# A four-layer graph network on one core: two banks for the gathered rows, signals counted by quads, and sum and one-hots of a quad in one step

## The chip, the cores and the metric

The kernel runs on one core of one Trainium2 chip. The number that counts is the device time of a whole execution in microseconds; lower is better. Engines are named as in the profile: PE is TensorE (PEld its weight loads), DVE is VectorE, ACT is ScalarE, POOL is GpSimd, SP is SyncE.

## What is computed

12,500 nodes with 128 features each, 212,500 edges sorted by destination, and four graph layers one after the other, each of the form x = x + layer(relu(layernorm(x))). Every layer is a product of the nodes with small weights and one or two sums over the edges. Cut to what matters:

```python
# layer 0, twice (10 relations): mean over the edges of each (destination, relation)
sums = segment_sum(x[src], dst * NUM_REL + edge_type, N * NUM_REL)
cnt  = segment_sum(ones, dst * NUM_REL + edge_type, N * NUM_REL)
out  = einsum('nrd,rdo->no', (sums / max(cnt, 1)).reshape(N, NUM_REL, -1), w_rel) + x @ root + bias
# layer 1 (3 relations): one sum of table rows, weighted by the edge
hr = einsum('ni,rio->rno', feature, weight)
h  = segment_sum(hr[rel_type, src] * norm[:, None], dst, N)
# layer 2, twice: mean over the in-edges
agg = segment_sum(h[src], dst, N) / max(deg, 1)[:, None]
h   = agg @ Wl.T + bl + h @ Wr.T
# layer 3: rows times a filter made from 20 edge features, summed by the other end of the edge
Wij = (ssp(f_ij @ W_filt1 + b_filt1) @ W_filt2 + b_filt2) * rcut_ij[:, None]
agg = segment_sum(h[idx_j] * Wij, idx_i, N)
```

## The kernel before

**Stages.** Dense stages and passes over the edges take turns. A dense stage reads the sums of the pass before (kept transposed in the SBUF tile `acc`, 128 features by 12,800 nodes), updates x and writes a table of rows to DRAM (`table_dram`). The seven passes are, in order, COUNT (pass 0, counts per relation, no table), LOOKUP (pass 1), four PLAIN passes (2 to 5) and FILTER (pass 6). Passes 1 to 5 are the gather passes: for each edge they fetch its table row. Pass 5 also prepares, for pass 6, where each edge's sum will be stored (`finds_dest`). The loop over repeats (`reps`) runs once for these inputs.

**One gather pass.** The edges are cut into 1664 tiles of 128, four tiles to a quad, four quads to a group, 104 groups. A group goes like this:

- POOL copies eight row numbers (`row_st` from `row_i`, L583), waits for the copy (`row_staged`), and issues eight indirect DMAs (L588), each of which fetches 128 rows of 512 bytes into one tile of `rows`; then the same for the other eight tiles. `rows` holds one group. So before each half POOL waits until PE has used the same half of the group before: `mm_done`, which PE raises by one after each tile.
- DVE waits until PE has done the whole group before, copies the destinations and weights of the group (`rw_st`, L1015 and L1032), and builds sixteen 128x128 one-hot tiles `hot` (they live in the tile `tab_s`), L1038: column n of edge e is the edge's weight if e goes to node n of the quad's window, else zero. Each raises `hot_ready` by one.
- PE waits for a quad's rows (`row_in[q]`) and one-hots and sums `rows` times `hot` over four tiles in one PSUM bank (L734; an f32 product is issued as two matmuls).
- DVE adds each quad's PSUM bank to a window of `acc` (L997) and raises `add_done` by four.

In the PLAIN passes DVE's order within a group is all sixteen one-hots and then the four additions. The LOOKUP pass is longer: an edge's weight (one over the count of its destination and relation) is not known yet. PE transposes small relation one-hots (L791), ACT copies them (L682), PE looks up the counts with them (L801, L803), and DVE multiplies and reduces each tile twice, first for the degree and then for the relation (`weigh`, L1050, an operation and the read of its accumulator), the second in place over `hot`. In pass 5 DVE also compares every tile's sources with each other (`pairs`, L1069, and their reduction, L1080), on rows that SP loads from DRAM by quads (`src_row`, L456).

**FILTER.** Pass 6 has its own order; POOL scatters with adding (L570), 16 tiles a group, each with waits of its own.

**What sets the order.** Everything is written out by hand: every engine runs its own loops, and semaphores with running counts join them. `settle` is a semaphore increment by the engine's sequencer after a wait.

Of the kernel before, what the change touches and what calls it, by code (L numbers as in the profile page):

```python
# [28 lines left out]
P = 128  # L29
# [34 lines left out]
def build(nc, d, out, n_nodes, n_edges):  # L64
# [34 lines left out]

    with ExitStack() as ctx:  # L100
# [22 lines left out]
        scratch = sb("scratch", [P, max(nacc, 3 * GROUP * P + 8 * BANK + 2 * P, 2 * COPIES * SB)])  # L123
        src_i = sb("src_i", [P, ntiles], I32)
        row_i = sb("row_i", [P, ntiles], I32)
# [109 lines left out]
        row_in = [sem(f"row_in{q}") for q in range(4)]  # L235
# [81 lines left out]
        def tiles_before(reps, pn):  # L317

            return reps * (pn * ntiles)

        def windows(e, g):
# [3 lines left out]
                skip_runtime_bounds_check_because="a destination or the start of a window of nodes, from 0 to n_nodes")[1]  # L325

# [58 lines left out]
        def _(sp):  # L385
# [10 lines left out]
            sp.wait_ge(add_done, reps * ntiles + GROUP)  # L396
# [11 lines left out]
            for k, p in enumerate(DENSE):  # L408
# [40 lines left out]
                if k == 1:  # L449
                    sp.wait_ge(add_done, reps * (3 * ntiles) + GROUP)  # L450
# [8 lines left out]
                if k == 4:  # L459
                    sp.wait_ge(add_done, tiles_before(reps, 5) + GROUP)  # L460
# [5 lines left out]
                if k == 5:  # L466

                    sp.wait_ge(add_done, tiles_before(reps, 6) + GROUP)
# [36 lines left out]
        def _(pool):  # L505
# [28 lines left out]
            for k, p in enumerate(DENSE):  # L534
# [21 lines left out]
                if PASSES[k + 1] != FILTER:  # L556
                    pool.wait_ge(rows_ready, sum(q in (0, 2, 3) for q in range(k + 1)))
                else:

                    with pool.Fori(0, reps) as r:  # L560
                        with pool.Fori(0, ngroups) as g:
                            n0 = pool.snap((r * ngroups + g) * 4)
                            base = pool.snap(tiles_before(reps, 6) + n0 * QUAD)
                            for q in range(4):
                                pool.wait_ge(dest_ready, n0 + (q + 2))
                                pool.wait_ge(add_done, base + (GROUP + QUAD * (q + 1)))
# [144 lines left out]
        def _(pe):  # L711
# [25 lines left out]
            def gathered(base, q):  # L737

                pe.wait_ge(row_in[q], base + 64)
# [166 lines left out]
        def _(dve):  # L906
# [92 lines left out]
            def run_pass(pn):  # L999
# [7 lines left out]
                with dve.Fori(0, reps) as r:  # L1007
                    set_windows(pn, r)
                    with dve.Fori(0, ngroups) as g:
# [89 lines left out]
                        if kind == LOOKUP:  # L1099
                            for u in range(GROUP):  # L1100
                                one_hot(u)
# [236 lines left out]
```

## Time and profile before

| | us |
|---|---|
| median of three runs | 18440.12 |
| lowest and highest run | 18428.23, 18442.12 |
| span of the profiled execution | 18422.2 |
| PE, DVE, ACT, POOL busy in it | 8433.5, 7139.1, 2442.5, 11077.2 |

The span runs from the first to the last instruction of the profiled execution; the median lies 17.9 us above it. Busy time counts the instructions themselves, not semaphore waits or register work. In rows with square brackets these hold the idle time just before the instruction and what ended it; such rows begin with the start and the duration. Rows of groups give busy time, the mean in ns of one, the idle time just before them and what ended it. Rows of waits give the total, how often, and the longest. A releaser "remote" means that no instruction of this core was found that ended the wait at that time; "issue" means that the profile shows nothing that was waited for.

### The profile page before, as it was taken

What the parts mean: (1) busy time and instruction counts of PE and PEld (TensorE: products, weight loads), DVE (VectorE), ACT (ScalarE), POOL (GpSimd) and SP (SyncE); (2) the same over time, 40 slices, a digit from 0 to 9 for tenths busy, and PEclk for the clock granted to TensorE, in tenths of its full rate; (3) what the DMA queues carried; (4) which work ended last, traced back from release to release, by engine and by line L of the source; (5) the groups of instructions that cost most, each with busy time, mean ns of one, the idle gap of its engine ahead of it and who ended that gap; (6) DMA issues with size and microseconds to landing.
All of it is one profiled execution on the core that took longest, in us unless ns stands there. A gap on an engine that the chain in (4) does not pass through costs nothing. (4 is left out here: it accounts for less than half of the span.)

```text
span 18422.2 us, 189911 instructions
## 1 busy us (share of the span) xinstructions
PE 8433.5 (46%) x37745; PEld 6706.7 (36%) x37746; DVE 7139.1 (39%) x33414; ACT 2442.5 (13%) x4374; POOL 11077.2 (60%) x11347
## 2 busy tenths in 40 slices
PE   2464444463333343333343333333333377777777
PEld 1233333333333333333332332322222355555555
DVE  7644444432222232222232222255555534444443
ACT  0120000020000020000020000000000044444443
POOL 0045555636666646666636666566666448888883
PEclk9975555585555565555565555555555567777775
DMA  2131111131111131111121111123333246666665
GB/s 85 64 123 40 40 39 39 40 146 55 45 45 45 45 100 45 45 45 45 45 66 45 45 45 45 49 80 84 83 84 84 73 95 118 118 117 118 117 117 122
DMA packets 981246, 1326.79 MB, mean 72 GB/s; under 512 B 201421, under 2 KB 635620, under 8 KB 981180
## 3 DMA queue, kind: packets, MB, share of 16 engines
q0 software_dynamic: 552016, 851.84, 21.1%
q1 hardware_dynamic: 429208, 474.72, 8.9%
q8 instruction: 6, 0.10, 0.0%
q14 instruction: 16, 0.13, 0.0%
HBM read 992.21 MB, written 333.54 MB: 72 GB/s over the span
## 5 line engine op out<-in xcount | busy, mean ns | idle before, releaser
L588 POOL DMA_INDIRECT rows<-table_dram,row_st x8320 | 8018.1, 964 | 3188.8 <-issue 2894.6
L734 PE MATMUL ps<-tab_s,rows 128*128 128x128 f32 x16640 | 4123.4, 427 | 6939.1 <-DMA rows<-table_dram,row_st 4302.8
L734 PEld LDWEIGHTS ps<-tab_s,rows 128*128 128x128 f32 x16640 | 3604.2, 320 | 7432.5 <-issue 7386.0
L570 POOL DMA_INDIRECT agg_dram<-acc,sum_row x1664 | 2646.9, 1591 | 529.0 <-issue 383.7
L997 DVE TENSOR_TENSOR acc<-ps,acc 128x128 f32 x2080 | 605.5, 291 | 5685.4 <-PE ps L734 4010.6
L1038 DVE TENSOR_SCALAR tab_s<-iota,rw_st 128x128 f32<-128x128 f32 x6656 | 1787.8, 361 | 11.5
L734 PE MATMUL ps<-scratch,tab_s 128*128 128x128 f32 x3328 | 669.0, 366 | 821.8 <-DVE scratch L1182 791.5
L583 POOL COPY row_st<-row_i 128x8 int32 x1040 | 210.5, 202 | 1262.7 <-PE ps L734 1072.4
L734 PEld LDWEIGHTS ps<-scratch,tab_s 128*128 128x128 f32 x3328 | 596.8, 269 | 871.7 <-issue 871.3
L548 POOL DMA_DIRECT2D table_dram<-tab_s x200 | 106.6, 533 | 1179.9 <-ACT tab_s L671 917.4
L635 ACT ACTIVATE yT<-acc 128x512 f32 x75 | 46.9, 626 | 4899.5 <-DVE acc L997 4893.7
L1176 DVE COPY sum_row<-etype 128x4 int32 x416 | 81.3, 195 | 1458.4 <-POOLq L569 1400.8
L1050 DVE CUSTOM_DVE_ANT_0 xs<-ps,tab_s 128x128 f32<-128x128 f32 x1664 | 385.1, 287 | 629.2 <-remote 446.2
L825 PE MATMUL ps<-scratch,acc 128*128 128x128 f32 x3328 | 593.3, 338 | 10.1 <-issue 5.9
L682 ACT ACTIVATE yT<-ps 128x512 bf16<-128x512 f32 x416 | 248.4, 597 | 2519.3 <-remote 1111.3
L1069 DVE TENSOR_SCALAR xn_h<-scratch,src_st 128x128 f32<-128x128 int32 x1664 | 377.5, 299 | 517.9 <-remote 392.0
L752 PE MATMUL ps<-scratch,wfilt 20*128 20x512 f32 x836 | 553.1, 745 | 35.0 <-DMA scratch<-in_feat 27.7
L825 PEld LDWEIGHTS ps<-scratch,acc 128*128 128x128 f32 x3328 | 559.2, 253 | 17.4 <-issue 17.4
L1050 DVE CUSTOM_DVE_ANT_0 tab_s<-ps,tab_s 128x128 f32<-128x128 f32 x1664 | 384.6, 287 | 457.5 <-remote 389.8
L551 POOL DMA_DIRECT2D table_dram<-tab_s x100 | 75.5, 755 | 795.6 <-ACT tab_s L671 609.7
L760 PEld LDWEIGHTS ps<-wfilt,scratch 128*128 128x128 f32 x3336 | 510.4, 219 | 15.8
L760 PE MATMUL ps<-wfilt,scratch 128*128 128x128 f32 x3336 | 507.3, 302 | 0.0
(182 smaller groups left out, 10596.4 us busy)
## 6 DMA issues: line engine op xcount, KB each, us to landing
scratch<-in_src_row SPq DMA_DIRECT2D x832, 256.0 KB
rows<-table_dram,row_st POOLq DMA_INDIRECT x8320
table_dram<-tab_s POOLq DMA_DIRECT2D x200, 640.0 KB, 3.2
scratch<-in_dst_row SPq DMA_DIRECT2D x416, 256.0 KB
scratch<-table_dram SPq DMA_DIRECT2D x416, 64.0 KB
agg_dram<-acc,sum_row POOLq DMA_INDIRECT x1664
scratch<-agg_dram SPq DMA_DIRECT2D x100, 256.0 KB, 3.8
x_dram<-xn_h SPq DMA_DIRECT2D x75, 256.0 KB, 2.4
```

Of the source, the lines that this page charges most:

```text
L570: pool.indirect_dma_start(agg_dram[j], bass.IndirectOffsetOnAxis(ap=sum_row[:, QUAD * q + j:QUAD * q + j + 1], axis=0), sums[:, q, j * P:( ...
L583: pool.tensor_copy(row_st[:, us[0]:us[-1] + 1], row_i[:, bass.ds(g * GROUP + us[0], GROUP // 2)]).then_inc(row_staged, 1)
L588: pool.indirect_dma_start(rows[:, u, :], None, table_dram[p["rels"]], bass.IndirectOffsetOnAxis(ap=row_st[:, u:u + 1], axis=0)).then_inc(r ...
L682: act.activation(rel_hotT[:, q % 2, :], ps[4][:], ACT.Copy).then_inc(relT_ready, 1)
L734: pe.matmul(o, lhs[:, u, :], rhs[:, u, :], start=j == 0 or not summed, stop=j == QUAD - 1 or not summed).then_inc(mm_done, 1)
L752: pe.matmul(ps[4][:], wfilt1[:], feat[:, q, :], start=True, stop=True).then_inc(f1_mm, 1)
L760: mm = pe.matmul(ps[6 + b][:, j * P:(j + 1) * P], f_buf[:, 2, b, j * P:(j + 1) * P], W["wfilt2"][:], start=False, stop=j == QUAD - 1)
L825: mm = pe.matmul(ps[5][:, j * P:(j + 1) * P], hotT[:, q % 2, j * P:(j + 1) * P], nodes[:, q % 2, :], start=True, stop=True)
L997: dve.tensor_tensor(window, ps[q][0:m, 0:P], window, ALU.add).then_inc(add_done, QUAD)
L1038: dve.tensor_scalar(hot[:, u, :], iota[:], rw_st[:, 0, u:u + 1], rw_st[:, 1, u:u + 1], ALU.is_equal, ALU.mult).then_inc(hot_ready, 1)
L1050: dve.tensor_tensor_reduce(out=out, in0=looked_up, in1=hot[:, u, :], scale=1.0, scalar=0.0, op0=ALU.mult, op1=ALU.add, accum_out=wout_st[: ...
L1069: i = dve.tensor_scalar(pairs[:, j, :], src_row[:, q, j * P:(j + 1) * P], src_st[:, u:u + 1], None, ALU.is_equal)
```

## The change

It has these parts.

- **Two banks of rows.** `row_banks` holds `rows` and 2048 columns of `scratch`. Groups use them in turn. POOL, PE and DVE loops over groups run two groups per iteration in the gather passes (`groups_by_bank`). Before group g, POOL waits until PE has finished group g-2 (with 104 groups `apart` is 2), once for the whole group instead of once for each half.
- **Row numbers by DVE.** POOL's two copies of row numbers per group go. DVE copies the 16 row numbers of group g+1 (`stage_rows`) while it works on group g; POOL waits for `row_staged`. The first group's are copied after DVE has prepared the pass's windows.
- **Quads are counted.** `mm_done`, `hot_ready`, `add_done` and `deg_step` rise by one for each quad, on the quad's last instruction, and `hot_made` once for a group. Before, all were raised by every tile (`add_done` by four for each quad).
- **PLAIN passes: one step for a quad.** DVE adds quad q of group g-1 and then builds the one-hots of quad q of group g, in the same place. Destinations and weights have two banks too (`rw_st2`). DVE no longer waits for the whole group before. In pass 5 the comparison of the quad's sources comes after its one-hots; before, it came ahead of them.

What COUNT and FILTER do is the same, with the new counts.

POOL, one group of the LOOKUP pass. `table_dram` is the table in DRAM. Before:

```order
L583 ISA [waits mm_done]
L583 COPY row_st<-row_i 128x8
L585 ISA
L588 DMA rows<-table_dram,row_st 128x128 [waits row_staged]
L588 DMA rows<-table_dram,row_st 128x128 x7
L581 REGISTER_ALU
L583 ISA [waits mm_done]
L583 COPY row_st<-row_i 128x8
```

Now, two groups:

```order
L593 ISA [waits row_staged]
L597 DMA rows<-table_dram,row_st 128x128 [waits mm_done]
L597 DMA rows<-table_dram,row_st 128x128 x15
L592 ISA
L593 ISA [waits row_staged]
L597 DMA scratch<-table_dram,row_st 128x128 [waits mm_done]
L597 DMA scratch<-table_dram,row_st 128x128 x15
```

Before, a copy and a wait for PE stood ahead of each eight DMAs; now sixteen DMAs stand in a row, no copy is between them, and every other group goes to `scratch`.

DVE, a group of the first PLAIN pass, from its first wait on (`ps` stands for the PSUM banks of the four quads). Before:

```order
L1015 ISA [waits mm_done]
L1015 COPY rw_st<-rel_dst 128x16
...
L1032 COPY rw_st<-wt_a 128x16
...
L1038 TENSOR_SCALAR tab_s<-iota,rw_st 128x128 [waits rw_staged]
L1038 TENSOR_SCALAR tab_s<-iota,rw_st 128x128 x15
...
L997 ISA [waits add_done,mm_done]
L997 TENSOR_TENSOR acc<-ps,acc 128x128
L994 REGISTER_ALU
L997 ISA [waits add_done,mm_done]
L997 TENSOR_TENSOR acc<-ps,acc 128x128
```

Now:

```order
L1113 COPY rw_st<-rel_dst 128x16
...
L1017 ISA [waits add_done,mm_done]
L1017 TENSOR_TENSOR acc<-ps,acc 128x128
L1127 TENSOR_SCALAR tab_s<-iota,rw_st 128x128 x4
L1014 REGISTER_ALU
L1015 REGISTER_ALU [waits mm_done]
L1017 ISA [waits add_done]
L1017 TENSOR_TENSOR acc<-ps,acc 128x128
L1127 TENSOR_SCALAR tab_s<-iota,rw_st 128x128 x4
...
L1031 COPY row_st<-row_i 128x16
```

The additions belong to the group before, and each is followed by the four one-hots that take its quad's place; the copy of row numbers comes last.

DVE, start of a LOOKUP group, now:

```order
L1031 ISA [waits mm_done]
L1031 COPY row_st<-row_i 128x16
L1078 ISA
L1078 COPY rw_st<-rel_dst 128x16
L1079 REGISTER_ALU
L1079 COPY rw_st<-etype 128x16
L1080 ISA
L1082 TENSOR_TENSOR xn_h<-rw_st,iota 128x16x10 [waits rw_staged]
L1082 TENSOR_TENSOR xn_h<-rw_st,iota 128x16x10 x2
L1087 TENSOR_SCALAR tab_s<-iota,rw_st 128x128 x16
L1089 ISA
L1091 ISA [waits hot_made]
```

Only the copy of row numbers is new; the wait for PE's whole group before stays here, and so does the order of all that follows.

The diff, cut to its core:

```diff
+    rows_at = 3 * GROUP * P + 6 * BANK
+    pairs_of = (ngroups + 1) // 2, ngroups // 2
+    apart = 2 if ngroups % 2 == 0 else 1
...
+        row_banks = [rows, scratch[:, rows_at:rows_at + GROUP * P].rearrange("p (u c) -> p u c", u=GROUP)]
-        row_st = sb("row_st", [P, GROUP], I32)
-        rw_st = sb("rw_st", [P, 2, GROUP])
+        row_st = sb("row_st", [P, 2, GROUP], I32)
+        rw_st2 = sb("rw_st", [P, 2, 2, GROUP])
+        rw_st = rw_st2[:, 0]
...
+        def groups_by_bank(e, body):
+
+            with e.Fori(0, ngroups // 2) as i:
+                body(i * 2, 0, i)
+                body(i * 2 + 1, 1, i)
+            if ngroups % 2:
+                body(ngroups - 1, 0, ngroups // 2)
...
-                    with pool.Fori(0, ngroups) as g:
+
+                    def gather(g, bank, i):
                         turn = pool.snap(reps * (k * ngroups) + r * ngroups + g)
-                        used = pool.snap(reps * ntiles + turn * GROUP)
-                        for part in range(2):
-
-                            pool.wait_ge(mm_done, used + (part + 1) * (GROUP // 2))
-                            us = range(part * (GROUP // 2), (part + 1) * (GROUP // 2))
-                            pool.tensor_copy(row_st[:, us[0]:us[-1] + 1],
-                                             row_i[:, bass.ds(g * GROUP + us[0], GROUP // 2)]).then_inc(row_staged, 1)
-                            pool.wait_ge(row_staged, turn * 2 + (part + 1))
-                            settle(pool)
-                            for u in us:
+                        used = pool.snap(reps * (4 * ngroups) + turn * 4)
+                        pool.wait_ge(row_staged, (reps * k + r) * (ngroups + 1) + g + 1)
+                        pool.wait_ge(mm_done, used + 4 * (3 - apart))
+                        settle(pool)
+                        for q in range(4):
+                            for u in range(QUAD * q, QUAD * (q + 1)):
                                 pool.indirect_dma_start(
-                                    rows[:, u, :], None, table_dram[p["rels"]],
-                                    bass.IndirectOffsetOnAxis(ap=row_st[:, u:u + 1], axis=0)
-                                ).then_inc(row_in[u // QUAD], 16)
+                                    row_banks[bank][:, u, :], None, table_dram[p["rels"]],
+                                    bass.IndirectOffsetOnAxis(ap=row_st[:, bank, u:u + 1], axis=0)
+                                ).then_inc(row_in[bank][q], 16)
+
+                    groups_by_bank(pool, gather)
...
-                pe.wait_ge(add_done, base + QUAD * (q + 1))
-                pe.wait_ge(hot_ready, base + QUAD * (q + 1))
+                pe.wait_ge(add_done, base + (q + 1))
+                pe.wait_ge(hot_ready, base + (q + 1))
                 for u in range(QUAD * q, QUAD * (q + 1)):
                     j = u % QUAD
                     o = ps[q][0:m, 0:P] if summed else ps[q][0:m, j * P:(j + 1) * P]
-                    pe.matmul(o, lhs[:, u, :], rhs[:, u, :], start=j == 0 or not summed, stop=j == QUAD - 1 or not summed
-                              ).then_inc(mm_done, 1)
+                    mm = pe.matmul(o, lhs[:, u, :], rhs[:, u, :], start=j == 0 or not summed,
+                                   stop=j == QUAD - 1 or not summed)
+                mm.then_inc(mm_done, 1)
...
+                    def stage_rows(g, bank):
+
+                        dve.tensor_copy(row_st[:, bank, :], row_i[:, bass.ds(g * GROUP, GROUP)]).then_inc(row_staged, 1)
...
+                    def one_hots(q, hot_of):
+
+                        for j in range(QUAD):
+                            i = hot_of(QUAD * q + j)
+                        i.then_inc(hot_ready, 1)
...
+                        for u in range(GROUP):
+                            i = dve.tensor_scalar(hot[:, u, :], iota[:], rw_st[:, 0, u:u + 1], None, ALU.is_equal)
+                        i.then_inc(hot_made, 1)
...
+                    def plain_group(g, bank, first, last):
...
+                        for q in range(4):
+                            if first:
+                                dve.wait_ge(mm_done, base + (q + 5))
+                            else:
+                                add_quad(before, win, q, acc, P)
+                            one_hots(q, lambda u: dve.tensor_scalar(hot[:, u, :], iota[:], rw[:, 0, u:u + 1],
+                                                                    rw[:, 1, u:u + 1], ALU.is_equal, ALU.mult))
+                            if finds_dest:
+
+                                dve.wait_ge(src_in[q], quads * 4 + 16)
...
+                        stage_rows(g + 1, 1 - bank)
```

## Rows read from the trace of the kernel before

**Rows 1.** The page: busy shares, POOL by slices, the groups of gathers and scatters.

```profile
PE 8433.5 (46%) x37745; PEld 6706.7 (36%) x37746; DVE 7139.1 (39%) x33414; ACT 2442.5 (13%) x4374; POOL 11077.2 (60%) x11347
...
POOL 0045555636666646666636666566666448888883
...
L588 POOL DMA_INDIRECT rows<-table_dram,row_st x8320 | 8018.1, 964 | 3188.8 <-issue 2894.6
...
L570 POOL DMA_INDIRECT agg_dram<-acc,sum_row x1664 | 2646.9, 1591 | 529.0 <-issue 383.7
```

**Rows 2.** Gathers (L588) alone by windows: length, POOL busy, PE clock, DMA share, GB/s.

```profile
1117.60:3874.40 2756.80, 1610.18 (x1664) 0.58 0.15 40
4171.10:6598.60 2427.50, 1594.89 (x1664) 0.50 0.17 45
...
12014.10:14623.90 2609.80, 1614.51 (x1664) 0.50 0.30 83
sum 12657.40, POOL 8018.10; mean POOL 1603.62
```

**Rows 3.** Groups of POOL: pass 1's copies, pass 2's gathers and copies, pass 5's copies.

```profile
L583 POOL COPY row_st<-row_i 128x8 int32 x207 | 40.0, 193 | 468.8 <-PE ps L734 434.5 <-remote 33.8
...
L588 POOL DMA_INDIRECT rows<-table_dram,row_st x1664 | 1594.9, 958 | 637.6 <-issue 594.2 <-POOL row_st L583 42.8 <-remote 0.3
L583 POOL COPY row_st<-row_i 128x8 int32 x207 | 40.7, 197 | 155.1 <-PE ps L734 134.9 <-remote 19.3 <-issue 0.3
...
L583 POOL COPY row_st<-row_i 128x8 int32 x207 | 47.2, 228 | 311.5 <-PE ps L734 240.3 <-remote 64.3 <-issue 5.8
```

**Rows 4.** Timeline of POOL in pass 3: inside a half, and between halves.

```profile
7506.31 0.95 POOL L588 DMA_INDIRECT rows<-table_dram,row_st  x1 [0.30 <-issue]
7507.27 0.20 POOL L583 COPY row_st<-row_i 128x8 int32 x1
7508.27 0.97 POOL L588 DMA_INDIRECT rows<-table_dram,row_st  x1 [0.81 <-issue]
```

**Rows 5.** Timeline of POOL in pass 1: a gather in the middle of a half.

```profile
2515.13 0.96 POOL L588 DMA_INDIRECT rows<-table_dram,row_st  x1 [2.03 <-issue]
```

**Rows 6.** Timeline, start of pass 2.

```profile
4171.83 1.89 DVE L987 TENSOR_TENSOR rel_dst<-dst_i,rel_dst 128x1664 f32<-128x1664 int32 x1
4172.51 2.07 POOL L588 DMA_INDIRECT rows<-table_dram,row_st  x1 [0.30 <-issue]
...
4174.78 0.17 DVE L1015 COPY rw_st<-rel_dst 128x16 f32 x1 [1.00 <-DVE win L988]
```

**Rows 7.** Timelines of PE and of DVE in one group of pass 3.

```profile
7609.68 2.04 PE L734 MATMUL ps<-tab_s,rows 128*128 128x128 f32 x8 [3.80 <-DMA rows<-table_dram,row_st]
7614.66 2.05 PE L734 MATMUL ps<-tab_s,rows 128*128 128x128 f32 x8 [2.94 <-DMA rows<-table_dram,row_st]
...
7607.59 4.19 DVE L1038 TENSOR_SCALAR tab_s<-iota,rw_st 128x128 f32<-128x128 f32 x16
7619.71 0.29 DVE L997 TENSOR_TENSOR acc<-ps,acc 128x128 f32 x1 [7.92 <-remote]
7626.81 0.29 DVE L997 TENSOR_TENSOR acc<-ps,acc 128x128 f32 x1 [6.81 <-PE ps L734]
```

**Rows 8.** Pass 1: window, busy (count) of PE, PEld, DVE, ACT, POOL; DVE's two largest waits.

```profile
1117.60:3874.40 2756.80, 1164.83 (x7034) 994.02 (x7034) 1340.04 (x9422) 247.19 (x415) 1650.09 (x1871) 0.58 0.15 40
...
DVE xs L1050 <- remote: 446.2, 126, 9.0
DVE tab_s L1050 <- remote: 385.5, 127, 4.9
```

**Rows 9.** The same of pass 5 (waits: us in total, times, longest).

```profile
12014.10:14623.90 2609.80, 845.93 (x3312) 736.22 (x3312) 1422.42 (x7771) 0.00 (x0) 1661.61 (x1871) 0.50 0.30 83
...
DVE xn_h L1069 <- remote: 392.0, 96, 7.0
...
DVE acc L997 <- remote: 125.7, 38, 6.3
```

More of the change, by code:

```diff
@@ L555, in _ @@
                 wait_stores(pool, k)
[L556 to L558 removed]
+                if PASSES[k + 1] == FILTER:
                     with pool.Fori(0, reps) as r:
@@ L832, in run_pass @@
                                 quad_products(base, q, same, P, msg, summed=False)
+                    if kind in (LOOKUP, PLAIN):
+                        groups_by_bank(pe, group)
+                    else:
+                        with pe.Fori(0, ngroups) as g:
+                            group(g)
             run_pass(0)
@@ new lines, in weigh, with lookup_group @@
+                    def weigh(q, w, looked_up, out, accum_sem):
+                        for j in range(QUAD):
+                            u = QUAD * q + j
+                            i = dve.tensor_tensor_reduce(
+                                out=out(u), in0=looked_up(j), in1=hot[:, u, :], scale=1.0, scalar=0.0,
+                                op0=ALU.mult, op1=ALU.add, accum_out=wout_st[:, w, u:u + 1])
+                        i.then_inc(accum_sem, 1)
+                    def lookup_group(g, bank, i):
+                        turn = dve.snap((reps * pn + r) * ngroups + g)
+                        base = dve.snap(turn * 4)
@@ L1119, in run_pass @@
[L1119 to L1124 removed]
+                        dve.tensor_copy(rw_st[:, 1, :], etype[:, bass.ds(g * GROUP, GROUP)]).then_inc(rw_staged, 1)
+                        dve.wait_ge(rw_staged, turn * 2 + 2)
@@ new lines, in lookup_group @@
+                        i.then_inc(hot_made, 1)
+                        dve.wait_ge(hot_made, r * ngroups + g + 1)
+                        for q in range(4):
+                            dve.wait_ge(look_mm, quads + (q + 3))
+                            weigh(q, 1, lambda j: ps[7][:, 0:P], lambda u: junk[:, u % QUAD, :], deg_step)
+                            if q >= 2:
+                                add_quad(base, win, q - 2, acc, P)
+                            dve.wait_ge(deg_step, quads + (q + 1))
+                            dve.sem_inc(deg_done, 1)
+                            weigh(q, 0, lambda j: ps[5 + q % 2][:, j * P:(j + 1) * P], lambda u: hot[:, u, :], hot_ready)
@@ new lines, in run_pass @@
+                    if kind == COUNT:
+                        with dve.Fori(0, ngroups) as g:
+                            count_group(g)
+                    elif kind == LOOKUP:
+                        groups_by_bank(dve, lookup_group)
+                    else:
+                        plain_group(0, 0, True, ngroups == 1)
+                        middle = (ngroups - 2) // 2 if ngroups > 2 else 0
+                        if middle:
+                            with dve.Fori(0, middle) as i:
+                                plain_group(i * 2 + 1, 1, False, False)
+                                plain_group(i * 2 + 2, 0, False, False)
+                        for g in range(1 + 2 * middle, ngroups):
+                            plain_group(g, g % 2, False, g == ngroups - 1)
```

251 lines of the change are left out of this document (115 added, 136 removed).

## The prediction

> **What bounds the kernel now.** I read the page first. No engine is busy throughout: POOL leads with 60% of the span, and its slices stand at 5 to 6 tenths through the middle of the program and at 8 in the scatters at the end [rows 1]. The gather group (L588) holds 8018.1 us of work, 964 ns each, and 3188.8 us of idle time just before gathers. Then the windows of the five gather passes, from the first gather's start to the last one's end: 12,657.4 us in all, 69% of the span, of which passes 3 and 4, by difference, take 2431.7 each, like pass 2 [rows 2]. Divided by 104 groups that is 26.5 us a group in pass 1, 23.3 in pass 2 and 25.1 in pass 5. The DMA share is 0.15 to 0.30, so the transfers themselves don't set the pace.
>
> Next, what POOL's group consists of. A gather takes 0.95 us and the next starts 0.30 us later, with nothing that was waited for; at a half there is a copy of 0.20 us and then 0.81 us before the next gather [rows 4]. On top, the copy waits for PE: 468.8 us in pass 1, 155.1 in pass 2 (taken for 3 and 4 too), 311.5 in pass 5 [rows 3]. So in the PLAIN passes POOL is nearly the bound, with stalls at its halves; in pass 1 and in pass 5 it stands behind the chain of DVE and PE. Since POOL reuses `rows` as soon as half of the group before is summed, POOL and that chain also stop each other. Scatters run at 1591 + 529.0/1664 ns = 1.91 us each, group boundaries with their waits included [rows 1]: a boundary whose waits are already satisfied adds nothing to the 0.3 us.
>
> **POOL's part, taken by itself.** The 1035 copies go (5 x 207 in the groups, at about 0.2 us: 205 us). The gap behind each shrinks from 0.81 to 0.30: 0.51 x 1035 = 528 us. The waits for PE go if group g-2 is always done in time: 468.8 + 3 x 155.1 + 311.5 = 1246 us. Together 1979 us. The check from the other side: 8018.1 of gathers + (3188.8 - 528) idle = 10,679 us, against 12,657 now. That is 20.5 us a group, call it the gather bound. The occasional gap of 2.03 us inside a half [rows 5] (75 of them in the five passes) is in the 3188.8; no wait of the program stands there, and I keep it: 75 x 1.73 = 130 us, which is the low end should they vanish.
>
> Why the wait for PE should go in the PLAIN passes: PE finishes a quad about 2 us after it begins it, and begins it on its rows' arrival [rows 7]. The bank that POOL wants next was last used by group g-2, whose rows were all issued one whole group, 20.5 us, before. DVE's new order makes quad q's one-hots right after adding quad q of the group before, so PE needs nothing of DVE that isn't a whole group old. DVE's work in pass 5 is 1422.4/104 = 13.7 us a group [rows 9], PE's 845.9/104 = 8.1; both fit in 20.5.
>
> **Lateness.** Row 7 shows a thing against easy sums: PE's second quad ended at 7616.71, and DVE's addition of it came at 7626.81; its first ended at 7611.72 and was added at 7619.71. So signals reach DVE up to 10 us late, beside a burst of 16 one-hots which each raise a semaphore. In PLAIN after, a group has 4 + 4 + 4 signals of the kind where it had 36, and 10 us of lateness against a slack of 20.5 - 2.04 leaves 8 us. I cost it at nothing there. If this cover is gone, POOL would stall by some 4 us a group (rival 2): 7.92 us [rows 7] in every second one.
>
> **LOOKUP.** Its order stays, and DVE still waits for the whole group before. DVE is busy 1340.0/104 = 12.9 us a group and waits the rest; of that 446.2 + 385.5 = 832 us, 8.0 a group, is "remote", that is late signals with no engine found behind them [rows 8]. Without them the chain is 26.5 - 8.0 = 18.5 us, under the gather bound. A group's increments fall from about 85 to 34: `mm_done` from 16 to 4, the one-hots' from 16 to 1, `deg_step` and `hot_ready` from 16 to 4 each. I take lateness in proportion: 8.0 x 34/85 = 3.2, so 21.7 us, 1.2 over the bound: +125 us. Between nothing (+0) and unchanged lateness (26.5: (26.5 - 20.5) x 104 = +624) I choose this because in the PLAIN group, too, the late signals stand beside the burst. The trace has no group with few signals, so this is the weakest term.
> By the Trainium skill, page "TensorE: Matmul & The Clock Gate", section "The cost: per-tile semaphore tail", a signal on each tile costs about 26 ns more than one on the last. No row here isolates that; 51 fewer signals would be 1.3 us a group by it, LOOKUP 25.2 us, and the term +489 instead of +125.
>
> **Pass 5.** DVE's remote waits are (392.0 + 125.7)/104 = 5.0 us a group, so its chain without them is 25.1 - 5.0 = 20.1 us; it now also has a group's slack. I take 20.5, and +312 (23.5 us a group) as the upper end, where half of the waits and of the delay stays.
>
> **Small terms.** The first gather of a pass now waits for DVE's windows: in pass 2 the first copy of DVE's group starts at 4174.78, after 1.89 us of window work that stretched a gather of POOL to 2.07 us beside it [rows 6]; there gathers start 3.6 us later (4174.8 instead of 4171.2), and I put the five passes at +30 us, the others' windows being longer. DVE's copy of row numbers, 0.2 us a group, is hidden behind its waits; in LOOKUP it lies on the chain, 104 x 0.2 = 21 us, and I count it within the 125. Gathers beside DVE work hardly stretch: 958 ns in pass 2 with 4.2 us of one-hots a group, 970 in pass 5 with 13.7 of DVE work. Were POOL locked out by every one-hot, 4.19 x 520 = 2180 us would be lost, yet the 964 ns already run beside them. COUNT, dense stages and FILTER (scatter bound) stay: 0, give or take 50.
> The Trainium skill, page "SBUF — State Buffer", section "🔬 SBUF: two separate sides", says that a VectorE copy in its two-port mode keeps GpSimd from writing descriptors. The 2.07 us gather agrees, the mean of 958 ns does not extend it to one-hots; by it the staging copies now made by DVE would cost at most 0.2 x 520 = 104 us.
>
> **Sum.** 18,440.1 - 1979 + 30 + 125 = 16,616 us; the span was 18,422.2, 17.9 below the median, and I carry that difference unchanged. Say 16,610.
>
> **Rivals.**
> 1. LOOKUP, and maybe pass 5, stay on the chain of DVE and PE. For it: remote waits have no engine behind them, so I can't know that fewer signals cure them; against it: the bursts beside them. LOOKUP alone unchanged: 16,610 - 125 + 624 = 17,110; with pass 5 at 23.5, 17,420. The figure by the skill's tail model, 16,610 - 125 + 489 = 16,975, lies here.
> 2. The banks bring no overlap in PLAIN, since late `mm_done` signals still stall POOL. With 7.92/2 = 4.0 us a group in passes 2 to 5: 16,610 + 4.0 x 104 x 4 = 18,270. With all the waits kept and only copies and gaps saved (205 + 528): 17,710 to 17,740.
> 3. Slower. POOL now never pauses, and every hand-off between DVE, PE and ACT in LOOKUP becomes late. Two hand-offs a quad at the present mean lateness of 3.5 us (446.2/126) and 3.0 (385.5/127) are 4 x 6.5 = 26 us, so the group takes 18.5 + 26 = 44.5 us and the total is 16,610 + 22.8 x 104 = 18,980. It decides from 39.3 us a group on, where four in five of the hand-offs are late; now it is 253 of 832. Against it: the lateness comes in pass 3 while POOL is itself waiting.
> 4. The change does less than it says: `apart` or the shared bank keeps POOL at group g-1. The order shows the wait and the second bank, so hardly.
>
> **Chances.** Forecast (16,400 to 16,800) 57%; rival 1 27%; rival 2 10%; no change 2%; slower 4%. The likeliest gives 16,610. The range must leave out at most 2 in 10: from 16,390 (rare gaps and most of the 125 gone) to 17,200 (LOOKUP unchanged, with 90 for the small terms). A difference of 0.2% is about what a measurement of this kernel can tell from no change. Faster 94%, same 2%, slower 4%.
>
> **What would show it.** In the profile after: gathers with 0.30 us before each and no copies on POOL; windows of 2120 to 2150 us in passes 2 to 5 and 2250 in pass 1; POOL at 7 to 8 tenths in the gather slices; DVE's remote waits in LOOKUP at about 3 us a group; the gather's mean at 960 to 970 ns. Wrong would be: waits for PE left ahead of L597 (rival 2), LOOKUP over 25 us (rival 1), gathers over 1.0 us beside DVE (then the bound itself moves, 83 us for each 10 ns).

## The result, and the profile after

The changed kernel took 18,981.7 us (median of four runs, 18,944.4 to 19,022.2) where the kernel before took 18,441.1: 1.0294 times as long, interval 1.0278 to 1.031. I had forecast 16,610. It is slower, and by the mechanism to which I had given 4%.

The profiled execution has a span of 19,020.4 us. Page of the changed kernel: POOL's slices, the two halves of the gather group (by bank), and two of DVE's groups (busy, mean ns, idle before and its releaser).

```profile
POOL 0034444443666664666646666656666628888883
...
L597 POOL DMA_INDIRECT scratch<-table_dram,row_st x4160 | 3998.8, 961 | 2729.7 <-issue 1265.4
L597 POOL DMA_INDIRECT rows<-table_dram,row_st x4160 | 3997.0, 961 | 2532.1 <-issue 1932.1
...
L1017 DVE TENSOR_TENSOR acc<-ps,acc 128x128 f32 x2080 | 606.4, 292 | 5977.3 <-remote 3909.8
...
L1066 DVE CUSTOM_DVE_ANT_0 xs<-ps,tab_s 128x128 f32<-128x128 f32 x1664 | 384.5, 288 | 1468.7 <-remote 1293.5
```

The copies are gone from POOL, and its gathers take what they took (961 ns against 964 [rows 1]). But the idle time before them grew from 3188.8 to 5261.8 us, and in pass 1 POOL fell from 5 tenths to 4. DVE's additions now wait for "remote" in most of their idle time, where before it was PE.

The gathers alone by windows, passes 1 to 5 (length, POOL busy, PE clock, DMA share, GB/s), the same view as [rows 2]:

```profile
1139.30:4387.60 3248.30, 1600.92 (x1664) 0.55 0.13 34
4703.10:7127.80 2424.70, 1594.42 (x1664) 0.50 0.17 45
7346.20:9790.60 2444.40, 1594.73 (x1664) 0.51 0.17 45
10018.80:12478.30 2459.50, 1594.14 (x1664) 0.51 0.17 44
12593.70:15220.90 2627.20, 1611.51 (x1664) 0.50 0.30 83
sum 13204.10, POOL 7995.73; mean POOL 1599.15
```

Against the kernel before, LOOKUP lost 491 us (31.2 us a group instead of 26.5), the PLAIN passes 2 to 4 lost 38 together, and pass 5 lost 17. Of the 598 us that the span grew, 547 lie here; 51 lie between the passes.

Inside a group the gathers go at 1.26 us from the first to the sixteenth. Nearly all of POOL's added idle time stands in one place, ahead of the first gather of a group. Waits of POOL in pass 1, then of DVE (total, times, longest):

```profile
POOL rows L597 <- issue: 652.2, 816, 13.2
POOL scratch L597 <- DVE row_st L1031: 569.5, 50, 12.0
...
DVE xs L1066 <- remote: 1280.3, 101, 26.4
DVE acc L1017 <- PE ps L745: 211.3, 158, 2.2
```

POOL waits some 11 us ahead of each group for DVE's row numbers, and DVE waits about once a group for a signal that comes from no work at that time: 12.3 us a group, and 1.0 more ahead of its second reductions, against 8.0 before [rows 8]. The timeline of one LOOKUP group shows what that wait is.

```profile
2519.25 0.53 PE L804 MATMUL ps<-ident_b,xn_h 128*128 128x128 bf16 x3
...
2530.25 0.95 POOL L597 DMA_INDIRECT rows<-table_dram,row_st  x1 [0.30 <-issue]
2533.23 0.29 DVE L1066 CUSTOM_DVE_ANT_0 xs<-ps,tab_s 128x128 f32<-128x128 f32 x1 [13.79 <-remote]
...
2534.06 0.60 ACT L693 ACTIVATE yT<-ps 128x512 bf16<-128x512 f32 x1 [16.42 <-remote]
...
2542.58 0.95 POOL L597 DMA_INDIRECT scratch<-table_dram,row_st  x1 [11.37 <-DVE row_st L1031]
```

PE ended the lookups of a quad at 2519.35 and the next transposes at 2519.78. DVE waits for the first and ACT for the second. Neither moves for 14 us, while POOL issues the rest of its sixteen gathers. POOL's last one ends at 2531.20; 2.0 us later DVE moves, then ACT. Then the group is finished, and only then is POOL told of the next row numbers. Such a wait, which lasts well after the work it waits for has ended, is called a hold here. In this trace the holds and POOL's gathers take turns; that the run of gathers makes the hold is what the experiments have to show.

In a PLAIN pass the same shows in about every second group (PE, DVE and POOL, pass 3):

```profile
8375.95 2.05 PE L745 MATMUL ps<-tab_s,scratch 128*128 128x128 f32 x8 [2.96 <-DMA scratch<-table_dram,row_st]
...
8382.07 0.29 DVE L1017 TENSOR_TENSOR acc<-ps,acc 128x128 f32 x1 [12.63 <-issue]
8398.87 0.29 DVE L1017 TENSOR_TENSOR acc<-ps,acc 128x128 f32 x1 [15.49 <-remote]
...
8393.38 0.95 POOL L597 DMA_INDIRECT rows<-table_dram,row_st  x1 [0.30 <-issue]
8401.23 0.95 POOL L597 DMA_INDIRECT scratch<-table_dram,row_st  x1 [6.90 <-DVE row_st L1031]
```

PE ended the last quad of a group at 8378.00. DVE added it at 8398.87, 20.9 us later (it had been free and waiting for 15.5 of them); that is 4.5 us after POOL stopped. POOL has no whole group of slack against this. It waits for the row numbers, and DVE copies them last in its group, after that addition and four one-hots. So some 14 us of lateness cost nothing (20.9 us late, and the gather starts 6.6 us later than it could), and what is above them POOL waits. By its start times, each of the 177 times that POOL waited ahead of a group in passes 2 to 4, 1,002 us together, it went on 0.9 to 1.1 us after that copy ended. The next group often goes without a long hold, and so on in turn.

Counted from when DVE was free and PE done, DVE went on more than 14 us late at 149 of its additions in passes 2 to 4 (the longest 20.1), at 125 of them while POOL stood still; of the 372 that were over 2 us late it was 174, so a hold can also end while POOL runs.

### The profile page after: what moved, and what is told of

Read it like the earlier page. It is cut to its first block, busy times and chain, and to the rows that moved or that the text cites. A ratio compares the mean times of both kernels' runs of the same rounds, so it can differ in the third digit from the quotient of the medians.

```text
span 19020.4 us, 184637 instructions
## 1 busy us (share of the span) xinstructions
PE 8494.8 (45%) x37745; PEld 6761.0 (36%) x37746; DVE 7085.7 (37%) x33940; ACT 2444.3 (13%) x4374; POOL 10847.9 (57%) x10307
## 4 chain that ended last, share of the span: by engine, by line
another core or an unknown queue 30%; DVE 20%; issue 18%; DMA 10%; PE 9%; POOL 7%; DVEq 2%; ACT 2%; POOLq 0%; ACTq 0%; SPq 0%
DMA agg_dram<-acc,sum_row 8%; DVE tab_s L1127 6%; POOL agg_dram L582 4%; PE ps L745 3%; DVE xn_h L1135 2%; POOL scratch L597 2%; DVE tab_s L1087 2%; PE ps L911 2%; DVE xn_h L1142 1%; DVE acc L1017 1%; PE ps L869 1%; POOL rows L597 1%; DVE tab_s L1056 1%; DVE xs L1066 1%
## 5 line engine op out<-in xcount | busy, mean ns | idle before, releaser
L597 POOL DMA_INDIRECT scratch<-table_dram,row_st x4160 | 3998.8, 961 | 2729.7 <-issue 1265.4
L597 POOL DMA_INDIRECT rows<-table_dram,row_st x4160 | 3997.0, 961 | 2532.1 <-issue 1932.1
L745 PE MATMUL ps<-tab_s,rows 128*128 128x128 f32 x8320 | 2105.2, 435 | 3527.5 <-DMA rows<-table_dram,row_st 2211.1
L745 PE MATMUL ps<-tab_s,scratch 128*128 128x128 f32 x8320 | 2093.7, 433 | 3451.4 <-DMA scratch<-table_dram,row_st 2395.2
L745 PEld LDWEIGHTS ps<-tab_s,rows 128*128 128x128 f32 x8320 | 1842.2, 326 | 3776.0 <-issue 3769.0
L745 PEld LDWEIGHTS ps<-tab_s,scratch 128*128 128x128 f32 x8320 | 1832.3, 325 | 3694.3 <-issue 3565.4
L1127 DVE TENSOR_SCALAR tab_s<-iota,rw_st 128x128 f32<-128x128 f32 x6656 | 1909.6, 361 | 238.3 <-issue 236.8
L562 POOL DMA_DIRECT2D table_dram<-tab_s x200 | 107.0, 535 | 1210.0 <-ACT tab_s L682 949.4
L814 PE MATMUL ps<-scratch,sel_deg 128*128 x416 | 118.9, 286 | 1340.1 <-DVEq L1096 679.0
L1142 DVE CUSTOM_DVE_ANT_0 xn_h<-xn_h,lower 128x128 f32<-128x128 f32 x1664 | 388.5, 289 | 440.8 <-remote 305.4
```

Of the source, the lines that this page charges most:

```text
L597: pool.indirect_dma_start(row_banks[bank][:, u, :], None, table_dram[p["rels"]], bass.IndirectOffsetOnAxis(ap=row_st[:, bank, u:u + 1], ax ...
L745: mm = pe.matmul(o, lhs[:, u, :], rhs[:, u, :], start=j == 0 or not summed, stop=j == QUAD - 1 or not summed)
L1127: one_hots(q, lambda u: dve.tensor_scalar(hot[:, u, :], iota[:], rw[:, 0, u:u + 1], rw[:, 1, u:u + 1], ALU.is_equal, ALU.mult))
L1142: i = dve.tensor_tensor_reduce(out=pairs_junk[:, j, :], in0=pairs[:, j, :], in1=lower[:], scale=1.0, scalar=0.0, op0=ALU.mult, op1=ALU.add ...
```

## The experiments

Two theories at the start. **A**: signals between DVE, PE and ACT are held while POOL issues gathers without a break, and the change made the unbroken run twice as long. **B**: the signals themselves are at fault, since now one a quad has to arrive where four did. Each kernel was timed beside the kernel before on its chip. In the six groups of runs (the last five on five different chips; the record does not name the first's) the kernel before took 18,441, 18,267, 18,430, 17,196, 18,374 and 17,192 us, and that turned out to be part of the answer. Windows of kernels from different groups compare across chips, and among the four slower ones the kernel before already varies by 174 us. The diffs are shortened.

**Three ways to break the run, and the signals put back** (kernel before: 18,267).

```diff
+ if q in (2,):          # pause_half; (1, 2, 3) in pause_quads
+     pool.tensor_copy(pause_st[:], row_st[:, bank, 0:8]).then_inc(paused, 1)
+     pool.wait_ge(paused, ...)
+ if q in (2,):          # drain_half, instead of that
+     pool.wait_ge(row_in[bank][q - 1], ...)
+ if j < QUAD - 1: mm.then_inc(more_pe, 1)    # more_signals, likewise on DVE
```

> The changed kernel, but POOL stops once in the middle of each group's sixteen gathers: it copies eight row numbers to a spare tile and waits for the copy, as it did at each half before. Theory A (signals between DVE, PE and ACT stay unseen while POOL issues gathers one after another, and come through when it pauses): LOOKUP falls from 31.3 us a group to 27 or less and the PLAIN passes from 23.4 to 22 or less, total 18,982 down to 18,100 or less, although the pause itself adds 0.7 us a group (73 us a pass). Theory B (fewer, quad-sized signals are at fault): windows unchanged or longer by up to 73 us each, total 19,000 to 19,350.

> The same with three pauses a group, one ahead of each quad but the first. Its own price is 3 x 0.7 = 2.1 us a group, so no gather pass can go under 20.5 + 2.1 = 22.6 us a group (2350 us). Theory A: no hand-off is later than one quad's 5 us; PLAIN 22.6 to 23 a group, LOOKUP 22.6 to 25, total 17,500 to 17,900, below the kernel before. Theory B: 19,000 to 20,000.

> The changed kernel, but in the middle of each group POOL waits until the rows of the quad it has just issued have landed, and issues nothing meanwhile (some 2 us, 200 us a pass). Tells what in a pause lets signals through. Theory A1 (POOL's not issuing): about as good as the short pause, plus 1.5 us a group, total about 18,300. Theory A2 (the landing of the rows holds the signals; only a stretch with no transfer in flight frees them): clearly better than the short pause in LOOKUP, whose longest waits then stay under 11 us, while the short pause leaves waits of 20 us and more.

> The changed kernel with the per-tile signals put back, on two semaphores that nobody waits for: every matmul of a quad, every one-hot and every reduction that had lost its increment raises one of them. Theory A (POOL's unbroken run): no change, 18,900 to 19,100. Theory B (per-tile signals had pushed late ones through): back to 18,440 or below. The rule that signals cost time by themselves: slower, by up to 51 x 26 ns = 1.3 us a group, 140 us in LOOKUP and as much as 60 in each other pass, 19,100 to 19,400.

Measured: `pause_half` 18,944.7 us (ratio 1.0372, 1.0354 to 1.0389), `pause_quads` 18,280.4 (1.0008, 0.9999 to 1.0018), `drain_half` 18,426.6 (1.0081, 1.0064 to 1.0098), `more_signals` 18,904.8 (1.0353, 1.0336 to 1.037). Windows of passes 1, 2 and 5 of `pause_quads`, then pass 1 of `drain_half`, passes 1 and 2 of `pause_half`, and pass 1 of `more_signals`:

```profile
1140.70:3873.00 2732.30, 1597.07 (x1664) 0.57 0.15 40
4187.00:6594.30 2407.30, 1588.02 (x1664) 0.50 0.17 45
11978.50:14460.20 2481.70, 1604.25 (x1664) 0.50 0.32 88
```

```profile
1141.10:3982.90 2841.80, 1602.27 (x1664) 0.57 0.15 38
```

```profile
1139.30:4247.80 3108.50, 1581.43 (x1664) 0.55 0.13 35
4564.60:7052.50 2487.90, 1576.04 (x1664) 0.52 0.17 44
```

```profile
1140.10:4361.80 3221.70, 1596.06 (x1664) 0.55 0.13 34
```

DVE's remote waits in pass 1 of `more_signals` (us in total, times, longest):

```profile
DVE xs L1072 <- remote: 1345.3, 110, 18.6
DVE tab_s L1072 <- remote: 39.2, 17, 2.3
```

More signals bring nothing back in LOOKUP (3222 us, 3248 without, and 13.3 us of remote waits a group in both): theory B had the kernel back at the time before, and it falls. The breaks do work there, and in order of how much POOL stands still: one of 0.7 us brings LOOKUP from 3248 us (3238 to 3249 in three traces of the changed kernel, none from this chip) to 3109, one of 2.0 us (all rows of the half landed) to 2842, three of 0.7 us to 2732. That last kernel pays 2.1 us a group for its pauses and is still some 3% faster than the changed one, by their ratios to the kernel before. But my expectations were too good. I had `pause_quads` at 17,900 us or less, and it only comes level with the kernel before; and one short break does not end a hold. In the PLAIN passes of `pause_half` holds of up to 20 us run on through the break, those passes are longer (2488 us) than without it, and the whole kernel is no faster than the changed one. Between POOL's standing still and the landing of the rows `drain_half` does not decide: it is much better than the short pause, but its longest remote wait in LOOKUP is 14.4 us, where I had said under 11.

**Is it a break as such, the bytes, or the other parts of the change?** (kernel before: 18,430)

```diff
- pool.wait_ge(mm_done, used + 4 * (3 - apart))   # old_waits, and at q in (0, 2):
+ pool.wait_ge(mm_done, used + (q + 6)), then the copy and its wait
+ pool.wait_ge(paused, turn * 3 + q)              # copy_quads: the copy of a group earlier
+ pool.tensor_copy(pause_st[...], ...).then_inc(paused, 1)
- row_banks[bank][:, u, :], None, table_dram[p["rels"]]
+ row_banks[bank][:, u, 0:8], None, table_dram[...] in rows of 8    # short_rows
```

> The changed kernel itself, beside the others on this chip. Both theories: 1.029 times the kernel before, LOOKUP 31.3 us a group, PLAIN 23.4 to 23.7.

> The changed kernel with its quad signals, its step of sum and one-hots and DVE's copies of row numbers, but POOL keeps to one group ahead of nothing: at each half it waits until PE has finished the same half of the group before, and makes a small copy there and waits for it, as before the change. Theory A (the unbroken run of gathers is at fault, not the signals and not DVE's order): LOOKUP back to 26 to 27 us a group (-490 us) and the other passes within 1% of the kernel before, ratio 0.99 to 1.005. If DVE's order or the quad signals did the harm: LOOKUP stays above 29.

> As the kernel with three pauses a group, but POOL doesn't wait for its copy: it waits for that of the group before, long done, so that the gap between two gathers at a quad's edge is the copy itself and about 0.3 us around it. If any break in the row of gathers is enough to let signals through: PLAIN 21.5 to 22.5 us a group and LOOKUP 25 to 26.5, ratio 0.97 to 0.985. If the length of the pause matters: LOOKUP 28 to 31, PLAIN 23 to 24, ratio 1.01 to 1.03.

> The changed kernel, but each gather fetches 128 rows of 32 bytes instead of 512, from other places of the table, so the sums are not the reference's; the number of gathers, of packets and of landing signals is the same. If the bytes in flight hold the signals up: LOOKUP below 25 us a group, PLAIN at the 20.5 us of the gathers, ratio below 0.93. If it is POOL's issuing or the number of transfers: windows within 3% of the changed kernel's, ratio 1.01 to 1.04.

Measured: `after_again` 18,961.0 us (1.0289, 1.0271 to 1.0306), `old_waits` 18,403.1 (0.9988, 0.9978 to 0.9997), `copy_quads` 19,153.9 (1.0395, 1.0378 to 1.0413), `short_rows` 19,015.1 (1.0312, 1.0294 to 1.0329). Windows of pass 1 of `old_waits`, of `copy_quads` and of `short_rows`:

```profile
1139.80:3899.20 2759.40, 1603.63 (x1664) 0.59 0.15 40
```

```profile
1139.70:4407.20 3267.50, 1597.01 (x1664) 0.55 0.13 33
```

```profile
1140.20:4402.60 3262.40, 1595.71 (x1664) 0.55 0.05 2
```

`old_waits` keeps the quad signals, DVE's new order and DVE's copies of row numbers, and gives POOL its old waits: LOOKUP is at 2759 us, where the kernel before has 2757 [rows 2], and the whole within 0.2%. `after_again`, on the same chip, has 3249. So all of the loss comes with POOL's freedom to run on (its old waits and its stops at the halves came back together here, so this run does not tell one from the other). `copy_quads` has as many extra copies as `pause_quads`, but POOL never waits for the one just made: it nearly hides in the 0.30 us between two gathers (1.31 us from gather to gather there). Nothing is gained, and the kernel is 193 us slower than `after_again`, most of it in the PLAIN passes; why is open. What mostly ends the long holds is POOL standing still, not an instruction of another kind. `short_rows` fetches 128 rows of 32 bytes from other places of the table, so its sums are not the reference's. With 2 GB/s instead of 34 the pass is as slow: the bytes in flight are not it.

**Let POOL stop by itself** (kernel before: 17,196). If a signal is late, PE is late, so a POOL that follows PE closely stops and frees it. The number in a name says how many quads before the next one PE need not have finished.

```diff
- pool.wait_ge(mm_done, used + 4 * (3 - apart))
  for q in range(4):
+     pool.wait_ge(mm_done, used + (q + 5))    # lead3; q + 4 in lead4, q + 6 in lead2
```

> The changed kernel, but ahead of every quad POOL waits until PE has finished the third quad before it, instead of the group before last once a group. POOL makes no copy; where signals are prompt, PE is done about 5 us before POOL asks. Theory A (a signal is held while POOL issues, so that a POOL that soon waits for it frees it): in PLAIN no late signal can last a whole group; windows of 2200 to 2330 us, LOOKUP 2600 to 2800, ratio 0.96 to 0.99. If what helped in the earlier kernels was only the copy and its wait: PLAIN at 2430 or more, ratio 1.0 to 1.03.

> The same with the fourth quad before. Theory A: late signals last a quad longer before POOL stops; between the kernel with three and the changed one, PLAIN 2300 to 2430 us, LOOKUP 2700 to 2900, ratio 0.98 to 1.0.

> The same with the second quad before, which is what the kernel before kept to at its halves. PE needs about 4.4 us after a quad's last gather is issued, a quad of gathers takes 5, so even prompt signals leave 0.6 us. Theory A: frequent short waits, PLAIN 2250 to 2420 us, LOOKUP 2600 to 2750, ratio 0.97 to 1.0.

> The changed kernel with one gather for each quad instead of four, so that three of four tiles are summed from rows that were not fetched; DVE, PE and ACT do all their work, with the same signals. POOL then issues for 5 us a group and waits for the rest. Theory A: DVE's remote waits in LOOKUP fall from 13.3 us a group to under 2, the pass takes 18 to 19 us a group (1,900 to 2,000 us), the PLAIN passes 8 to 11. If the late signals have nothing to do with the gathers: LOOKUP stays near 31 us a group, since POOL's 20 us of gathers are not what bounds it.

Measured: `lead3` 16,300.1 us, `lead4` 16,298.7, `lead2` 16,304.3 (ratios 0.9479, 0.9478, 0.9481, each within 0.0016), `quarter` 10,850.4 in a single run. The three were alike to 6 us, PLAIN passes 2 to 4 at 20.1 us a group, and DVE and ACT without a remote wait in the gather passes. Remedies of different strength would not do that, and the kernel before was 7% faster than elsewhere. So this chip had no late signals, and none of the expected differences could show. The granted TensorE clock is not the reason: in the PLAIN passes it is 0.50 here, as it is where signals are late. `quarter`, meant to show that the signals are late only beside gathers, can't show it there; what it gives is the chain of DVE, PE and ACT with few gathers, 16.3 us a LOOKUP group and 5.7 a PLAIN one, at a higher granted clock (0.71 in LOOKUP, against 0.65 in `after_fourth`).

**The same chip for all** (kernel before: 18,374, late signals).

> The changed kernel again, beside the kernel with a lead of three quads. If the chip is one with late signals (kernel before at 18,300 or more): 1.029 times the kernel before. If it has none (kernel before near 17,200): 16,300, ratio 0.948, every gather pass at 20.1 to 20.5 us a group, as the sum without late signals has it.

> POOL waits ahead of each quad for the third quad before it. On a chip with late signals: theory A says that a held signal stops POOL within three quads and so comes free; ratio 0.96 to 0.99. If the lead does nothing there: 1.0 to 1.04. On a chip without: 16,300, the same as the changed kernel.

> The kernel before, for a trace from this chip. On a chip with late signals: LOOKUP 26.5 us a group and remote waits of 800 us there, as in the first trace. On a chip without: LOOKUP near 23, PLAIN near 22.5 us a group, with the 0.8 us at each half left, and next to no remote waits.

Measured: `after_third` 18,967.8 us (1.0329, 1.0311 to 1.0346), `lead3_again` 18,503.8 (1.0072, 1.0055 to 1.0089), `before_profiled` 18,345.6. Windows of passes 1, 2 and 5 of `lead3_again`, then of the kernel before on this chip:

```profile
1140.30:4095.80 2955.50, 1602.64 (x1664) 0.62 0.14 37
4400.90:6792.50 2391.60, 1593.32 (x1664) 0.50 0.17 46
12127.70:14710.70 2583.00, 1612.06 (x1664) 0.50 0.31 84
```

```profile
1117.90:3860.90 2743.00, 1614.60 (x1664) 0.58 0.15 40
4160.30:6586.00 2425.70, 1602.72 (x1664) 0.50 0.17 45
11990.80:14550.20 2559.40, 1619.94 (x1664) 0.50 0.31 85
```

The lead of three quads takes 464 us off the changed kernel, less than theory A had promised (a ratio of 0.96 to 0.99): its PLAIN pass 2 beats that of the kernel before by 34 us, its LOOKUP stays 212 behind and pass 5 24.

**Both remedies together, and the changed kernel on a chip without late signals** (kernel before: 17,192).

```diff
  for q in range(4):
+     pool.wait_ge(mm_done, used + (q + 5))
+     if q > 0 and k in (0, 4):    # LOOKUP and pass 5; all passes in rest_all
+         the copy of pause_quads and its wait
```

> Lead of three quads in all passes; in LOOKUP and pass 5 also a copy and its wait on POOL ahead of each quad but a group's first. If the gains add: LOOKUP 26.3 us a group, PLAIN 23.0, pass 5 23.9; total about 18,500 - 220 - 100 = 18,180, ratio 0.99. If they don't add, LOOKUP stays at 28.5: ratio 1.005. On a chip without late signals: LOOKUP and pass 5 at 22.4, a ratio of 0.97 instead of 0.948.

> The same with the pauses in all five passes. PLAIN can't go under 20.1 + 2.1 = 22.2 us a group; with three pauses alone it took 23.2. If the lead adds to it: 22.4 to 22.9 and a ratio of 0.985 to 0.99; if not, 23.2 and 0.992. On a chip without late signals: 22.2 in each pass, ratio 0.99.

> The changed kernel. With late signals (kernel before at 18,200 or more): ratio 1.029 to 1.033. Without: 16,300 us, ratio 0.948.

Measured: `rest_first_last` 16,710.3 us (0.9717, 0.9701 to 0.9734), `rest_all` 17,434.5 (1.0145, 1.0129 to 1.0162), `after_fourth` 16,291.2 (0.9474, 0.9458 to 0.949). This chip again had no late signals, so the two combined kernels tell only the price of the pauses: 2.2 us a group, a pass of 2338 us instead of 2106. (I had expected `rest_all` at 0.99 on such a chip; that was wrong arithmetic, since 16,291 and five passes of 104 groups at 2.2 us make 17,435.) Whether they beat the kernel before on a chip with late signals stays open. The changed kernel by itself is the find. Its windows of the five gather passes:

```profile
1139.20:3245.70 2106.50, 1599.61 (x1664) 0.65 0.20 52
3546.00:5637.00 2091.00, 1584.21 (x1664) 0.50 0.20 52
5857.30:7949.10 2091.80, 1585.00 (x1664) 0.50 0.20 52
8174.10:10265.50 2091.40, 1584.60 (x1664) 0.50 0.20 52
10378.40:12500.40 2122.00, 1615.07 (x1664) 0.50 0.39 102
sum 10502.70, POOL 7968.48; mean POOL 1593.70
```

And its waits in pass 1, of POOL and of DVE:

```profile
POOL scratch L597 <- issue: 253.6, 832, 0.3
POOL rows L597 <- issue: 252.3, 828, 0.3
...
DVE acc L1017 <- PE ps L745: 542.3, 117, 5.8
DVE xs L1066 <- PE ps L816: 94.4, 137, 1.8
```

No wait of POOL is longer than its 0.3 us once the pass is under way, and DVE has no remote wait. The same program, with POOL busy 10,815.8 us (10,847.9 on the first chip) and DVE 7,051.6 (7,085.7), is 2,690 us shorter here than where signals are late.

## Why the prediction was wrong

**POOL's part was right.** Copies gone, 0.30 us before each gather, group boundaries free when their waits are satisfied. Where nothing is late the five windows sum to 10,503 us. My gather bound was 10,679; of the difference, 130 us are the gaps of 2.03 us [rows 5], which I kept and which did not appear there once, and 50 us are gathers of 958 instead of 964 ns.

**The step that failed is the paragraph on lateness.** I read in [rows 7] that a signal came 10 us late, saw a burst of one-hots beside it, and took the burst for the cause. From that came two terms. Both failed. For LOOKUP I scaled the 8.0 us of remote waits a group by the number of signals, to 3.2 and a group of 21.7 us; `more_signals` shows that the number does not matter, and the remote waits rose to 13.3 a group (1280.3 and 103.8 us) and the group to 31.2: +987 us against my sum. For the PLAIN passes I set a lateness of 10 us against a slack of 18 and put the cost at nothing. Both numbers were wrong. The 10 us were no property of a signal: they ended just after POOL had stopped for its own wait, and with a run twice as long they became 20.9. And the slack was 14 us, because POOL waits for DVE's copy of the row numbers, at the end of DVE's group. I had priced that copy as 0.2 us of work, hidden, and not as a wait of POOL on DVE, which the kernel before doesn't have. The passes took 2443 us instead of 2136, +921 in three. Pass 5 was held as well, 2627 instead of 2136, +491. The three make 2,399 of the 2,406 us between my sum of 16,616 and the profiled execution's 19,022.

**What the row said and I left unread.** In [rows 7] DVE woke at 7626.81. This is POOL's timeline there, in the kernel before:

```profile
7622.67 0.95 POOL L588 DMA_INDIRECT rows<-table_dram,row_st  x1 [0.30 <-issue]
7626.85 0.19 POOL L583 COPY row_st<-row_i 128x8 int32 x1 [3.23 <-PE ps L734]
```

POOL had stopped at 7623.62 and waited too; DVE and POOL both moved 3.2 us later. Of 296 additions in passes 2 to 4 of the kernel before that came over 2 us late, 154 came while POOL stood still, which it did for 11% of the time (the 0.30 us between gathers left out). A count of the late wakes by their place in POOL's run would have shown it. I had the thought in rival 3 ("POOL now never pauses, and every hand-off becomes late"), priced it in LOOKUP alone, and found that it decides only from 39.3 us a group. It did not have to reach that, because the same mechanism took the gain of the other four passes too. That rival 3 has 18,980 us, nearly what was measured, is luck: it puts 2,370 us above my sum into LOOKUP alone, where 987 were lost. A rival has to be priced in all the stages in which its mechanism works.

**Rival 2** was the right shape for PLAIN (stalls of POOL left at the boundary, 4.0 us a group in my price, 3.0 measured above the gather bound), rival 3 for LOOKUP. I had priced them apart. Together, with my own figure for PLAIN and pass 5 (+1,660) and LOOKUP at the 31 us that were measured (+970), they give 19,240.

**The page's rule** on the tail of per-tile signals: the Trainium skill, page "TensorE: Matmul & The Clock Gate", section "The cost: per-tile semaphore tail", would make 51 more signals a group cost 1.3 us, 140 us in LOOKUP. `more_signals` had 3222 us there, the changed kernel 3248. The page measured it on matmuls, and 39 of the 51 signals are DVE's. With the other passes I had expected 19,100 to 19,400 us from that price, and the kernel took 18,905. But the two kernels ran on different chips, and by their ratios to the kernel before `more_signals` (1.0353) lies 0.2 to 0.6% above the changed kernel, so a smaller price is not excluded.

**The gather of 2.07 us.** I took it as agreeing with what the Trainium skill, page "SBUF — State Buffer", section "🔬 SBUF: two separate sides", says of VectorE copies. What ran beside it was a subtraction of two tiles [rows 6], so that row bears on no copy. DVE's staging copies cost nothing that shows: where signals are prompt, the gathers of pass 2 take 952 ns each, against 958 before.

**A part that one trace could not show** is that the answer depends on the chip. Four comparisons of the changed kernel gave 1.029, 1.029, 1.033 and 0.947. The one trace I had came from a chip with late signals. Its 832 us of remote waits in pass 1 [rows 8] were the sign of it, but nothing said that they are absent elsewhere.

## What to carry to other kernels

A wait that the profile puts down to no engine is a resource of its own: find where in the neighbours' work it ends before taking away the pause that ends it. An engine that is freed to run on can be worth less than one that stops now and then, so when a change removes a producer's pauses, count each hand-off of the others that falls into its longer run, in every stage. A copy that is moved to another engine is also a new wait on that engine: no run here tells what the two banks give if the row numbers are copied at the start of DVE's group, or by POOL, and that is the first thing I would try. And compare on more than one chip before believing a gain or a loss of 3 to 5% in a kernel with such waits.

## What the runs showed of the hardware

- In four of the six groups of runs, signals from PE to DVE and ACT are held while POOL issues indirect gathers of 128 rows, one each 1.26 us: in the changed kernel DVE went on 8 to 15 us late in most LOOKUP groups (one 25), and 14 to 20 us late 149 times in passes 2 to 4. The longest holds mostly end 2 to 5 us after POOL stops. PE's own remote waits in pass 1 stayed at 4.8 us or less. One break of 0.7 us a group did little, one of 2.0 us or three of 0.7 us did more; a copy that POOL does not wait for, more signals, and shorter rows (2 instead of 34 GB/s) did not help.
- In the other two groups (two chips) there were no late signals. With late signals the kernel before takes 18,270 to 18,440 us, without them 17,190; the changed one 18,960 to 18,980 and 16,290. COUNT takes the same on both (the first gather of the changed kernel starts at 1139.3 and at 1139.2 us). No chip was met in two groups as far as the record tells, so a difference in time rather than between chips is not excluded. What holds a signal, and what the chips differ in, none of these runs shows.
- A gather of 128 rows costs POOL 0.96 us with rows of 512 bytes and 0.96 with rows of 32.
